# The first three query and key norms of a windowed attention kernel: their roots as a power on GpSimd

## The chip, the cores and the metric

The kernel runs on one core of a Trainium2 chip. The metric is the device time of one execution in microseconds (us). The core has five instruction streams that run side by side: TensorE (PE, with its weight loads PEld), VectorE (DVE), ScalarE (ACT), GpSimd (POOL) and SyncE (SP), which here issues the DMAs.

## The reference

One sequence of 4096 tokens of width 256 goes through windowed attention with 16 heads of 16 columns, then a layer norm, a feed-forward layer with binarized weights, and a second layer norm. What matters here is that each head's query and key are divided by their length:

```python
def _l2norm(t):
    n = jnp.sqrt(jnp.sum(t * t, axis=-1, keepdims=True))
    return t / jnp.maximum(n, EPS)

q = _l2norm(proj(Wq))
k = _l2norm(proj(Wk))
v = proj(Wv)
attn = jnp.einsum('bhqd,bhkd->bhqk', q, k)
...                                   # window of 128 keys, a fading bias, softmax
x = _layernorm(x + attention(x))
x = _layernorm(x + ffn(x))
```

## The kernel before

The tokens are cut into 32 blocks of 128. Block n goes through these stages, each written out by hand in the program of its engine; semaphores join them.

- PE projects queries and keys into one PSUM bank (`project_qk`), 512 columns.
- ACT squares them (`squares`, tile `sq`, L649); DVE sums each head's 16 squares (`sums_of`, tile `ss`, L948) and writes `half`, the sum bounded from below times -0.5 (L875). There are 32 sums in a row: 16 heads of queries and 16 of keys.
- The root: ACT takes the logarithm (L654) and the exponential (L656), which gives a first `rnorm`; DVE improves it by one Newton round of three instructions (`round_of`, L880, L882, L884).
- DVE multiplies the projections by `rnorm` (`normalise_rows`, tile `qkn`, L964).
- ACT writes the rounded 16-bit upper part of `qkn` into `parts` (`high_halves`, L665 queries, L668 keys). What the rounding lost goes beside it: in blocks 0 and 1 POOL subtracts for the queries (L1441) and DVE for the keys (`split_keys`, L927); in later blocks POOL does both (`low_halves`, L1425, L1427). DVE copies the queries' pair (`double`, L921).
- SP issues a transposing DMA from `parts` to `qkT` (`turn_parts`, L274), and PE multiplies queries and keys (`scores`, L391). ACT takes the exponential of the scores (L701), and POOL cuts the window out of them (L1407).

Before the regular steps there is an opening for blocks 0, 1 and 2: the program of each engine writes their stages out one behind the other. On DVE, the sum and `half` of block n+1 stand behind the normalisation of block n, then comes the key split of block n, then the round and the normalisation of block n+1. POOL is given nothing in the opening but two constant matrices and the two subtractions. In the opening one semaphore, `newton`, is raised six times for a root: by `half`, by the logarithm, by the exponential and by the three instructions of the round.

The rows of the page name lines of the kernel before.

Of the kernel before, what the change touches and what calls it, by code (L numbers as in the profile page):

```python
# [11 lines left out]
ALU = mybir.AluOpType  # L12
# [3 lines left out]
P = 128  # L16
# [4 lines left out]
H = 16  # L21
# [11 lines left out]
NORM_EPS = 1e-6  # L33
LN_EPS = 1e-5
QK_SCALE = 2.0 ** 10
# [7 lines left out]
NORM_OPS = 6  # L43
# [56 lines left out]
def count(sem_engine, sem, value):  # L100

    if isinstance(value, int) and value <= 0:
        return
    sem_engine.wait_ge(sem, value)


def norm_base(i, next3):

    return (i + 3) * NORM_OPS if next3 else NB * NORM_OPS + (i - NB + 3) * (NORM_OPS - 1) - 1


def norm_columns(next3, ln):

    return slice(0 if next3 else 2 * H, 2 * H + 1 if ln else 2 * H)


def build(nc, x, xT, wqkvT, woT, w1, w1T, b1c, w2T, b2, out):
    with ExitStack() as ctx:
        def sb(name, shape, dt=F32):
            return ctx.enter_context(nc.sbuf_tensor(name, shape, dt))  # L120

        def sem(name):
            return ctx.enter_context(nc.semaphore(name))
# [28 lines left out]
        ss = sb("ss", [P, 2 * H])  # L152
        half = sb("half", [P, 2 * H + 1])
# [3 lines left out]
        rnorm = sb("rnorm", [P, 2 * H + 1])  # L157
# [14 lines left out]
        yparts = sb("yparts", [P, 2, 2, DC, GB, P], F16)  # L172
        yT = sb("yT", [P, 2, 2, DC, GB, P], F16)
        mv_late = sb("mv_late", [P, LATE, 2])
        late_rstd = sb("late_rstd", [P, LATE])
        resid4 = resid[:].rearrange("p n (k t) -> p n k t", k=DC)

# [41 lines left out]
        qkproj_done, sq_done, ss_done, newton, qkn_done = (  # L219
            sem(n) for n in ("qkproj_done", "sq_done", "ss_done", "newton", "qkn_done"))  # L220
# [26 lines left out]
        znewton, z_ready = sem("znewton"), sem("z_ready")  # L247
        end_seed, end_log, end_guess, end_round, end_root = (
            sem(n) for n in ("end_seed", "end_log", "end_guess", "end_round", "end_root"))
        zlast_sum, rows_by_act, last_row = sem("zlast_sum"), sem("rows_by_act"), sem("last_row")  # L250
        stored = [sem("stored_even"), sem("stored_odd")]

# [391 lines left out]
        def _(act):  # L644
            def squares(n, par):

                act.wait_ge(qkproj_done, n + 1)
                count(act, ss_done, n)
                nc.scalar.activation(sq[:], ps[:, QK[par], :], ACT.Square, scale=1.0 / QK_SCALE).then_inc(sq_done, 1)  # L649

            def root(half_, ln_, y, done, base, seeded):

                act.wait_ge(done, base + seeded)
                nc.scalar.activation(ln_, half_, ACT.Ln, scale=-2.0).then_inc(done, 1)  # L654
                act.wait_ge(done, base + seeded + 1)
                nc.scalar.activation(y, ln_, ACT.Exp, scale=-0.5).then_inc(done, 1)  # L656

            def high_halves(n, par, first=False, again=False):

                act.wait_ge(qkn_done, n + 1)  # L660
                count(act, qk_in[par], 8 * (n - 2 - par) + 16 if not isinstance(n, int) or n >= 2 else 0)
                if again:
                    count(act, again_in, (n - 2) * (16 // XS))
                src = qkn[:, par, :].rearrange("p (h d) -> p h d", d=HD)
                made = nc.scalar.activation(parts[:, par, 0:H, 0, :], src[:, 0:H, :], ACT.Copy)  # L665
                if first:
                    made.then_inc(first_high, 1)
                nc.scalar.activation(parts[:, par, H:2 * H, 0:2, :],  # L668
                                     src[:, H:2 * H, :].unsqueeze(2).to_broadcast([P, H, 2, HD]),
                                     ACT.Copy).then_inc(hi_done, 1)  # L670
# [57 lines left out]
            def norm_of(i, next3, ln):  # L728
                base, cols = norm_base(i, next3), norm_columns(next3, ln)
                if not next3:  # L730
                    act.wait_ge(ln_seed, i - 3)
                root(half[:, cols], lnx[:, cols], rnorm[:, cols], newton, base, 1)
# [12 lines left out]
            act.wait_ge(layout, 4)  # L745
            nc.scalar.activation(fade_parts[:], fade_parts[:], ACT.Exp, scale=-1.0).then_inc(fade_made, 1)
            squares(0, 0)
            norm_of(-3, True, False)
            squares(1, 1)
            high_halves(0, 0, first=True)  # L750
            norm_of(-2, True, False)
            squares(2, 0)
            high_halves(1, 1, first=True)
            norm_of(-1, True, False)
            step(0, 0, strips=False, ln=False, both=False, high_first=True)
            step(1, 1, strips=False, ln=False, squares_first=True)
            step(2, 2, strips=False, ln=False, squares_first=True)
# [114 lines left out]
        def _(dve):  # L872
            def rsqrt_seed(s, half_, eps, op, done, scale=1.0):

                nc.vector.tensor_scalar(half_, s, eps, -0.5 / scale ** 2, op, ALU.mult).then_inc(done, 1)  # L875

            def rsqrt_round(half_, a, b, y, done, base):

                dve.wait_ge(done, base + 3)
                nc.vector.tensor_tensor(a, half_, y, ALU.mult).then_inc(done, 1)  # L880
                dve.wait_ge(done, base + 4)
                nc.vector.tensor_tensor(b, a, y, ALU.mult).then_inc(done, 1)  # L882
                dve.wait_ge(done, base + 5)
                nc.vector.scalar_tensor_tensor(out=y, in0=b, scalar=1.5, in1=y, op0=ALU.add,  # L884
                                               op1=ALU.mult).then_inc(done, 1)
# [54 lines left out]
                                                   fade[:, at, :].unsqueeze(2).to_broadcast([P, H, HD]), ALU.mult)  # L940
                made.then_inc(v_ready, 1)

            def sums_of(n, ln):

                base = norm_base(n - 3, True)
                dve.wait_ge(sq_done, n + 1)
                count(dve, newton, base - NORM_OPS + 1)
                nc.vector.tensor_reduce(ss[:], sq[:].rearrange("p (h d) -> p h d", d=HD), AX.X, ALU.add).then_inc(ss_done, 1)  # L948
                dve.wait_ge(ss_done, n + 1)
                count(dve, qkn_done, n)  # L950
                if ln:
                    dve.wait_ge(ln_seed, n - 6)
                rsqrt_seed(ss[:], half[:, 0:2 * H], (NORM_EPS / QK_SCALE) ** 2, ALU.max, newton)

            def round_of(i, next3, ln):

                cols = norm_columns(next3, ln)
                rsqrt_round(half[:, cols], nt_a[:, cols], nt_b[:, cols], rnorm[:, cols], newton, norm_base(i, next3))

            def normalise_rows(n, par):  # L960

                dve.wait_ge(newton, norm_base(n - 3, True) + NORM_OPS)
                count(dve, lo_done, n - 1)
                nc.vector.tensor_tensor(qkn[:, par, :].rearrange("p (h d) -> p h d", d=HD),  # L964
                                        ps[:, QK[par], :].rearrange("p (h d) -> p h d", d=HD),
                                        rnorm[:, 0:2 * H].unsqueeze(2).to_broadcast([P, 2 * H, HD]),
                                        ALU.mult).then_inc(qkn_done, 1)
# [91 lines left out]
                dve.wait_ge(bound_turned, 1)  # L1059
                nc.vector.tensor_reduce(bound_max[:], turned_at, AX.X, ALU.max).then_inc(bound_max_done, 1)  # L1060

            sums_of(0, False)
            round_of(-3, True, False)
            normalise_rows(0, 0)
            sums_of(1, False)
            split_keys(0)
            round_of(-2, True, False)
            normalise_rows(1, 1)
            dve.wait_ge(first_low, 1)
            sums_of(2, False)  # L1070
            split_keys(1)
            round_of(-1, True, False)
            normalise_rows(2, 0)
            dve.wait_ge(first_low, 2)
            fade_values(0, 0)
# [315 lines left out]
        def _(pool):  # L1391

            nc.gpsimd.iota(idx_i[:], pattern=[[0, 1]], base=0, channel_multiplier=1).then_inc(idx_made, 1)
            nc.gpsimd.memset(id16[:], 0.0).then_inc(id_zero, 1)
            nc.gpsimd.memset(id32[:], 0.0).then_inc(id_zero, 1)
            pool.wait_ge(id_zero, 2)
# [14 lines left out]
            def cut_chunk(i, c, slot, both=True):  # L1411

                own = cut_tile(i, c, slot, 0)
                if both:
                    cut_tile(i, c, slot, 1).then_inc(cut_ready, 1)
                else:
                    own.then_inc(cut_ready, 1)
# [13 lines left out]
            def step(i, slot, next2=True, both=True, low_at=2, behind=None):  # L1431
                for c in range(NC):
                    if next2 and c == low_at:
                        low_halves(i + 2, slot % 2)
                    cut_chunk(i, c, slot, both)
                if behind:
                    behind()

            for n in range(2):
                pool.wait_ge(first_high, n + 1)  # L1440
                nc.gpsimd.tensor_tensor(parts[:, n, 0:H, 1, :], qkn[:, n, 0:D].rearrange("p (h d) -> p h d", d=HD),  # L1441
                                        parts[:, n, 0:H, 0, :], ALU.subtract).then_inc(lo_done, 1)
            step(0, 0, both=False, low_at=0)
            step(1, 1, low_at=1)
            for n in range(2, 5):
# [97 lines left out]
```

## Time and profile before

| what | value |
|---|---|
| time, median of 3 runs | 371.64 us (370.44 to 371.90) |
| the profiled execution's own time | 370.31 us |
| its span in the trace | 368.5 us |
| PE busy | 354.4 us, 96% of the span |
| DVE, ACT, POOL busy | 324.7, 309.8, 273.2 us |
| part of the span that the change touches | about 8.5 to 16.4 us |

The profiled execution is one of its own, with its own time; the span is what lies between its first and last recorded instruction. A row of the timeline gives the start, the duration, the engine, the line, the operation, the tiles written and read with their shapes, and in brackets how long the engine had been idle and what ended that.

### The profile page before, as it was taken

To read this page: it belongs to the slowest core of one execution; us is meant where nothing else is said; L and a number is where in the kernel's file an instruction comes from. 1 tells how busy PE (TensorE), PEld (TensorE's weight loads), DVE (VectorE), ACT (ScalarE), POOL (GpSimd) and SP (SyncE) were. 2 spreads that over 40 slices of the span, in tenths; PEclk is the share of its full clock that TensorE was granted. 3 is DMA by queue.
4 is the path that set the end of the run, shared out by engine and by line. 5 is a ranking of instruction groups with operands and counts; after the bars stand their busy time and mean duration, and the time that the engine had idled before them with its cause. 6 is when DMAs were issued, how large, how long until landed. Compare 5 with 4: busy or idle time off the path is not lost. (4 is left out here: it accounts for less than half of the span.)

```text
span 368.5 us, 13159 instructions
## 1 busy us (share of the span) xinstructions
PE 354.4 (96%) x4461; PEld 244.6 (66%) x4461; DVE 324.7 (88%) x860; ACT 309.8 (84%) x539; POOL 273.2 (74%) x418
## 2 busy tenths in 40 slices
PE   8899999999999999999999999999999999999991
PEld 5555676667767766776776667765666666666780
DVE  5978899898898898898889998869889999999995
ACT  2598898888898898998899999988888898897773
POOL 1189999889989999999999999757474663764330
PEclk9999999999999999999999999999999999999997
DMA  7668854835654655767767863303303413413113
GB/s 221 152 139 183 167 117 89 171 85 115 137 119 89 139 118 110 158 148 164 146 166 137 170 130 62 58 4 59 59 0 60 114 58 58 115 48 68 57 60 114
DMA packets 106885, 40.20 MB, mean 109 GB/s; under 512 B 92128, under 2 KB 105824, under 8 KB 106720
## 3 DMA queue, kind: packets, MB, share of 16 engines
q1 hardware_dynamic: 106848, 39.73, 48.7%
q8 instruction: 20, 0.33, 0.4%
q14 instruction: 17, 0.14, 0.1%
HBM read 12.72 MB, written 4.19 MB: 46 GB/s over the span
## 5 line engine op out<-in xcount | busy, mean ns | idle before, releaser
L1407 POOL TENSOR_SCALAR_AFFINE_SELECT prob<-prob 128x512 f32<-128x512 f32 x252 | 153.0, 642 | 11.3 <-ACT prob L701 11.2
L701 ACT ACTIVATE prob<-ps 128x1024 f32<-128x1024 f32 (+1 forms) x128 | 122.1, 1008 | 12.9 <-PE ps L391 12.9
L552 PE MATMUL ps<-yT,sgn 128*128 128x512 f16 x256 | 61.1, 379 | 0.0
L773 ACT ACTIVATE ps<-ps,bias,alpha 128x512 f32<-128x512 f32 x64 | 47.8, 749 | 15.7 <-PE ps L552 12.5
L422 PE MATMUL ps<-wqkv,xt 128*128 128x512 f32 x124 | 58.7, 596 | 0.1
L1475 POOL TENSOR_TENSOR resid<-z,resid 128x256 f32 (+1 forms) x31 | 22.6, 729 | 46.0 <-DVE z L1191 46.0
L412 PE MATMUL ps<-prob,vdiag 128*17 128x128 f32 x1024 | 51.3, 274 | 0.2
L412 PE MATMUL ps<-prob,vnext 128*17 128x128 f32 x992 | 49.9, 273 | 0.0
L552 PEld LDWEIGHTS ps<-yT,sgn 128*128 128x128 f16 x256 | 25.0, 98 | 22.6
L455 PE MATMUL ps<-wo,oT 128*128 128x256 f32 x128 | 36.2, 405 | 0.1
L391 PE MATMUL ps<-qkT 64*64 64x192 f16 (+2 forms) x1024 | 34.0, 248 | 1.9 <-DMA qkT<-parts 1.4
L431 PE MATMUL ps<-wqkv,xt 128*128 128x256 f32 x128 | 34.4, 391 | 1.3 <-DMA wqkv<-in_wqkvT 0.8
L1427 POOL TENSOR_TENSOR parts<-qkn,parts 128x512 f16<-128x512 f32 x30 | 35.0, 1166 | 0.0
L391 PEld LDWEIGHTS ps<-qkT 64*64 64x64 f16 x1024 | 20.0, 105 | 20.1 <-issue 20.0
L422 PEld LDWEIGHTS ps<-wqkv,xt 128*128 128x128 f32 x124 | 21.2, 190 | 16.2 <-issue 15.4
L586 PE MATMUL ps<-sgn,w 128*128 128x256 f16 x256 | 30.6, 273 | 0.0
L412 PEld LDWEIGHTS ps<-prob,vdiag 128*17 128x17 f32 x1024 | 26.2, 97 | 5.9 <-issue 2.3
L586 PEld LDWEIGHTS ps<-sgn,w 128*128 128x128 f16 x256 | 25.1, 98 | 6.3
L586 PE MATMUL ps<-sgn,prob 128*128 128x256 f16 x240 | 28.5, 273 | 0.1
L412 PEld LDWEIGHTS ps<-prob,vnext 128*17 128x17 f32 x992 | 28.2, 98 | 0.0
L1457 POOL TENSOR_TENSOR yparts<-resid,yparts 128x256 f16<-128x256 f32 (+1 forms) x32 | 21.2, 682 | 8.8 <-ACT yparts L767 8.8
L586 PEld LDWEIGHTS ps<-sgn,prob 128*128 128x128 f16 x240 | 23.4, 98 | 5.6 <-DVE prob L1181 0.3
(119 smaller groups left out, 689.0 us busy)
## 6 DMA issues: line engine op xcount, KB each, us to landing
xt<-in_xT SPq DMA_DIRECT2D x32, 128.0 KB, 2.2
resid<-in_x SPq DMA_DIRECT2D x32, 128.0 KB, 2.2
out_dram<-resid SPq DMA_DIRECT2D x7, 512.0 KB, 2.9
w<-in_w2T SPq DMA_DIRECT2D x1, 1024.0 KB, 8.3
w<-in_w1T SPq DMA_DIRECT2D x4, 256.0 KB, 3.3
w_nat<-in_w SPq DMA_DIRECT2D x4, 256.0 KB, 3.3
wqkv<-in_wqkvT SPq DMA_DIRECT2D x3, 256.0 KB, 4.0
qkT<-parts SPq DMA_TRANSPOSE x39, 4.3
```

The lines of the kernel that those rows point to most:

```text
L391: mm = nc.tensor.matmul(ps[keys, SC + 2 * (c % 2) + hp, 2 * P * t + first:2 * P * t + last], qkT[row, H // 2 + 2 * c + t, slot, keys], row ...
L412: mm = nc.tensor.matmul(ps[32 * m:32 * m + HD + 1, OT, P * c:P * c + P], v, p, start=(n == 0), stop=(n == 1 or not near))
L422: mm = nc.tensor.matmul(ps[:, QK[slot % 2], :], xt[:, slot, k, :], wqkv[:, k, 0:2 * D], start=(k == 0), stop=(k == DC - 1))
L431: mm = nc.tensor.matmul(ps[:, VO, 0:D], xt[:, slot, k, :], wqkv[:, k, 2 * D:3 * D], start=(k == 0), stop=(k == DC - 1))
L455: mm = nc.tensor.matmul(ps[:, VO, D:2 * D], oT[:, k, :], wo[:, k, :], start=(k == 0), stop=(k == DC - 1))
L552: mm = nc.tensor.matmul(ps[:, bank, :], sgn1[:, c, P * k:P * k + P], yT[:, par, a, c, :, :], start=(m == 0), stop=(m == 2 * DC - 1))
L586: mm = nc.tensor.matmul(ps[:, banks[b], 0:D], hid[par][:, a, k, P * b:P * b + P], sgn2[:, k, :], start=(m == 0), stop=(m == 2 * HC - 1))
L701: nc.scalar.activation(to, scored, ACT.Exp, scale=QK_SCALE ** -2).then_inc(exp_done, 1)
L773: nc.scalar.activation(bank, bank, ACT.Gelu, bias=bias1[:, k:k + 1], scale=alpha1[:, k:k + 1]).then_inc(gelu_done, 1)
L1407: return nc.gpsimd.affine_select(out=at, in_=at, compare_op=ALU.is_ge, fill=0.0, base=-near, pattern=[[0, CH], [1 if near else -1, P]], ch ...
L1427: nc.gpsimd.tensor_tensor(parts[:, par, H:2 * H, 2:4, :], src[:, H:2 * H, :].unsqueeze(2).to_broadcast([P, H, 2, HD]), parts[:, par, H:2 * ...
L1475: nc.gpsimd.tensor_tensor(resid[:, m, :], z[:, b, :], resid[:, m, :], ALU.add).then_inc(zsum, 1)
```

## The change

For blocks 0, 1 and 2 the six instructions of the root behind `half` become one on POOL: `rnorm` is the bounded sum to the power -0.5, taken elementwise over 128 x 32 numbers. `half` then holds the bounded sum without the factor -0.5. ACT's logarithms and exponentials and DVE's rounds of these blocks are gone (6 instructions and 9). POOL fills a tile with -0.5 once, and raises `newton` by five with its power, so that everything counts on as before. Block 3 and later keep the old root.

```diff
@@ scalar: the opening
             squares(0, 0)
-            norm_of(-3, True, False)
             squares(1, 1)
             high_halves(0, 0, first=True)
-            norm_of(-2, True, False)
             squares(2, 0)
             high_halves(1, 1, first=True)
-            norm_of(-1, True, False)
@@ vector: sums_of
-                rsqrt_seed(ss[:], half[:, 0:2 * H], (NORM_EPS / QK_SCALE) ** 2, ALU.max, newton)
+                if powered:
+                    nc.vector.tensor_scalar(half[:, 0:2 * H], ss[:], (NORM_EPS / QK_SCALE) ** 2, None,
+                                            ALU.max).then_inc(newton, 1)
+                else:
+                    rsqrt_seed(ss[:], half[:, 0:2 * H], (NORM_EPS / QK_SCALE) ** 2, ALU.max, newton)
@@ vector: the opening
-            sums_of(0, False)
-            round_of(-3, True, False)
+            sums_of(0, False, powered=True)
             normalise_rows(0, 0)
-            sums_of(1, False)
+            sums_of(1, False, powered=True)
             split_keys(0)
-            round_of(-2, True, False)
             normalise_rows(1, 1)
             dve.wait_ge(first_low, 1)
-            sums_of(2, False)
+            sums_of(2, False, powered=True)
             split_keys(1)
-            round_of(-1, True, False)
             normalise_rows(2, 0)
@@ gpsimd
+            nc.gpsimd.memset(minus_half[:], -0.5).then_inc(halves_set, 1)
...
+            def first_root(n):
+
+                pool.wait_ge(newton, norm_base(n - 3, True) + 1)
+                count(pool, qkn_done, n)
+                nc.gpsimd.tensor_tensor(rnorm[:, 0:2 * H], half[:, 0:2 * H], minus_half[:],
+                                        ALU.pow).then_inc(newton, NORM_OPS - 1)
+
+            pool.wait_ge(halves_set, 1)
+            first_root(0)
             for n in range(2):
                 pool.wait_ge(first_high, n + 1)
                 nc.gpsimd.tensor_tensor(parts[:, n, 0:H, 1, :], qkn[:, n, 0:D].rearrange("p (h d) -> p h d", d=HD),
                                         parts[:, n, 0:H, 0, :], ALU.subtract).then_inc(lo_done, 1)
+                first_root(n + 1)
```

On POOL, at the opening of its program, the instructions before are these (the identity matrices `id`, the two subtractions for the queries of blocks 0 and 1, then those of block 2 and the window cuts):

```order
L1394 MEMSET id 128x128
L1395 MEMSET id 128x128
L1398 AFFINE_SELECT id<-id 128x128 x2
L1441 TENSOR_TENSOR parts<-qkn,parts 128x16x16 x2
L1425 TENSOR_TENSOR parts<-qkn,parts 128x16x16
L1427 TENSOR_TENSOR parts<-qkn,parts 128x16x32
```

and now:

```order
L1394 MEMSET minus_half 128x32
L1395 MEMSET id 128x128
L1396 MEMSET id 128x128
L1399 AFFINE_SELECT id<-id 128x128 x2
L1444 TENSOR_TENSOR rnorm<-half,minus_half 128x32
L1451 TENSOR_TENSOR parts<-qkn,parts 128x16x16
L1444 TENSOR_TENSOR rnorm<-half,minus_half 128x32
L1451 TENSOR_TENSOR parts<-qkn,parts 128x16x16
L1444 TENSOR_TENSOR rnorm<-half,minus_half 128x32
L1426 TENSOR_TENSOR parts<-qkn,parts 128x16x16
L1428 TENSOR_TENSOR parts<-qkn,parts 128x16x32
```

A power stands ahead of each of the two subtractions and one behind them, ahead of block 2's.

On DVE, the stretch from the sums of block 1 to the normalisation of block 1 reads before:

```order
L948 TENSOR_REDUCE ss<-sq 128x32
L875 TENSOR_SCALAR half<-ss 128x32
L927 TENSOR_TENSOR parts<-qkn,parts 128x16x32
L921 COPY parts<-parts 128x16x32
L880 TENSOR_TENSOR nt_a<-half,rnorm 128x32
L882 TENSOR_TENSOR nt_b<-nt_a,rnorm 128x32
L884 SCALAR_TENSOR_TENSOR rnorm<-nt_b,rnorm 128x32
L964 TENSOR_TENSOR qkn<-ps,rnorm 128x512
```

and now:

```order
L947 TENSOR_REDUCE ss<-sq 128x32
L953 TENSOR_SCALAR half<-ss 128x32
L926 TENSOR_TENSOR parts<-qkn,parts 128x16x32
L920 COPY parts<-parts 128x16x32
L967 TENSOR_TENSOR qkn<-ps,rnorm 128x512
```

The three instructions of the round are gone, and the key split of block 0 with its copy is all that still stands between `half` and the normalisation.

## Rows read from the trace of the kernel before

**Rows 1.** The page: span, busy time by engine, granted clock in 40 slices

```profile
span 368.5 us, 13159 instructions
...
PE 354.4 (96%) x4461; PEld 244.6 (66%) x4461; DVE 324.7 (88%) x860; ACT 309.8 (84%) x539; POOL 273.2 (74%) x418
...
PEclk9999999999999999999999999999999999999997
```

**Rows 2.** Windows: stretch, length, busy time of each engine, clock, DMA

```profile
17.00:60.00 43.00, 41.38 (x568) 26.44 (x568) 37.43 (x79) 38.05 (x67) 39.12 (x60) 1.00 0.71 149
60.00:200.00 140.00, 139.64 (x2264) 98.22 (x2263) 125.63 (x312) 124.60 (x218) 129.84 (x197) 1.00 0.61 131
```

**Rows 3.** Timeline of DVE and ACT, block 0, from half to the normalisation

```profile
8.35 0.18 DVE L875 TENSOR_SCALAR half<-ss 128x32 f32<-128x32 f32 x1
8.56 0.23 ACT L654 ACTIVATE lnx<-half 128x32 f32<-128x32 f32 x1 [0.97 <-DVE half L875]
9.53 0.19 DVE L884 SCALAR_TENSOR_TENSOR rnorm<-nt_b,rnorm 128x32 f32<-128x32 f32 x1
9.76 0.69 DVE L964 TENSOR_TENSOR qkn<-ps,rnorm 128x512 f32<-128x512 f32 x1
```

**Rows 4.** Timeline of DVE, block 1, from half to the normalisation

```profile
11.08 0.61 DVE L875 TENSOR_SCALAR half<-ss 128x32 f32<-128x32 f32 x1
11.61 0.68 DVE L927 TENSOR_TENSOR parts<-qkn,parts 128x512 f16<-128x512 f32 x1
12.21 0.28 DVE L921 COPY parts<-parts 128x512 f16<-128x512 f16 x1
...
13.07 0.69 DVE L964 TENSOR_TENSOR qkn<-ps,rnorm 128x512 f32<-128x512 f32 x1
```

**Rows 5.** Timeline of DVE, block 2, from half to the normalisation

```profile
14.39 0.61 DVE L875 TENSOR_SCALAR half<-ss 128x32 f32<-128x32 f32 x1
...
15.52 0.28 DVE L921 COPY parts<-parts 128x512 f16<-128x512 f16 x1
...
16.39 0.69 DVE L964 TENSOR_TENSOR qkn<-ps,rnorm 128x512 f32<-128x512 f32 x1
```

**Rows 6.** PE's waits up to 45 us, SP's timeline, and landing of the first two transposes

```profile
PE ps L391 <- DMA qkT<-parts: 1.4, 1, 1.4
...
12.58 5.16 SPq L274 DMA_TRANSPOSE qkT<-parts  x2
...
DMA to landing us min/median/max: 4.3/4.3/4.4
```

**Rows 7.** Timeline of ACT, from the first transpose's landing to block 3's squares

```profile
17.11 0.42 ACT L665 ACTIVATE parts<-qkn 128x256 f16<-128x256 f32 x1 [1.59 <-DVE qkn L964]
...
17.95 1.06 ACT L701 ACTIVATE prob<-ps 128x512 f32<-128x512 f32 x2
19.46 0.60 ACT L649 ACTIVATE sq<-ps 128x512 f32<-128x512 f32 x1 [0.44 <-PE ps L422]
```

**Rows 8.** Timeline of POOL up to 19 us

```profile
10.98 0.67 POOL L1441 TENSOR_TENSOR parts<-qkn,parts 128x256 f16<-128x256 f32 x1 [8.95 <-ACT parts L665]
14.29 0.67 POOL L1441 TENSOR_TENSOR parts<-qkn,parts 128x256 f16<-128x256 f32 x1 [2.64 <-ACT parts L665]
18.20 0.67 POOL L1425 TENSOR_TENSOR parts<-qkn,parts 128x256 f16<-128x256 f32 x1 [3.23 <-ACT parts L668]
```

**Rows 9.** POOL's groups by form: busy us, mean ns, idle before

```profile
L1407 POOL TENSOR_SCALAR_AFFINE_SELECT prob<-prob 128x512 f32<-128x512 f32 x252 | 153.0, 642 | 11.3 <-ACT prob L701 11.2
L1427 POOL TENSOR_TENSOR parts<-qkn,parts 128x512 f16<-128x512 f32 x30 | 35.0, 1166 | 0.0
L1425 POOL TENSOR_TENSOR parts<-qkn,parts 128x256 f16<-128x256 f32 x30 | 20.3, 678 | 8.5 <-ACT parts L668 8.4
...
L1398 POOL TENSOR_SCALAR_AFFINE_SELECT id<-id 128x128 f32<-128x128 f32 x1 | 0.3, 292 | 0.0
```

**Rows 10.** Timeline of DVE, a round's first instruction beside POOL's window cuts

```profile
27.73 0.61 DVE L880 TENSOR_TENSOR nt_a<-half,rnorm 128x32 f32<-128x32 f32 x1
```

More of the change, by code:

```diff
@@ L174, in build @@
         mv_late = sb("mv_late", [P, LATE, 2])
+        minus_half = sb("minus_half", [P, 2 * H])
         late_rstd = sb("late_rstd", [P, LATE])
@@ L249, in build @@
             sem(n) for n in ("end_seed", "end_log", "end_guess", "end_round", "end_root"))
+        halves_set = sem("halves_set")
         zlast_sum, rows_by_act, last_row = sem("zlast_sum"), sem("rows_by_act"), sem("last_row")
@@ L941, in fade_values, with sums_of @@
                 made.then_inc(v_ready, 1)
-            def sums_of(n, ln):
+            def sums_of(n, ln, powered=False):
                 base = norm_base(n - 3, True)
```

## The prediction

> **What bounds the kernel now.** I read the page first: of a span of 368.5 us PE is busy for 354.4, at a granted clock in the top tenth in every slice but the last [rows 1]. The windows say where the rest is: from 60 to 200 us PE is busy for 139.64 of 140 us, from 17 to 60 us for 41.38 of 43 [rows 2]. So behind the opening there is next to no idle time of PE into which a late start could vanish, and none from which an early start could be robbed: what the opening gains or loses at about 17 us, the end gains or loses, nearly one for one. The chain of waits on the page ends before it gets back to the opening, so this is an inference from busy time, not a reading of the chain.
>
> Then the opening. PE stands still for 1.4 us until the first transpose has landed; SP issued it at 12.58, as soon as the copy of block 0 was done, and it took about 4.3 us [rows 4, 6]. ACT stood still for 1.59 us before 17.11 and then rounds block 2 up to the exponentials of 17.95 [rows 7]. So two paths arrive at 17.1 us together: root 0, normalisation 0, key split 0, copy, transpose; and roots 0, 1 and 2 one behind the other on DVE, normalisation 2, rounding of block 2. The first has no slack. The second has 0.44 us, which is ACT's wait for PE's projection of block 3 before the squares at 19.46 [rows 7].
>
> **The change part by part.** I call P the duration of one power on POOL and work out each block in P.
>
> Block 0. Before, `half` ends at 8.53 and the normalisation starts at 9.76, 1.23 us later [rows 3]. Now there are a handover to POOL, the power, and a handover back. For the two handovers I take 0.07 and 0.04 us, from `half`'s end to the logarithm (0.03) and from the round's end to the normalisation (0.04) with some more for POOL [rows 3]. The shift is P + 0.11 - 1.23 = P - 1.12. DVE has nothing else to do meanwhile: the sums of block 1 stand behind the normalisation.
>
> Block 1. `half` ends at 11.69, and DVE goes straight to the key split of block 0 (L927) and the copy, which ends at 12.49 [rows 4]. Here the port matters. `half` took 0.18 us in block 0 and 0.61 in blocks 1 and 2, where it ran against a subtraction on POOL (10.98 to 11.65, 14.29 to 14.96) [rows 3, 4, 5, 8]; and a round's instruction takes 0.61 against the window cuts [rows 10]. So DVE's instructions and POOL's keep each other out. The key split is on DVE as soon as `half` ends, 0.07 us before POOL has its signal, so I take it that the split and the copy go first and the power behind them: 12.49 + P + 0.04 against 13.07 before, a shift of P - 0.54. If POOL gets in ahead of the copy instead, the normalisation comes out much the same, but the copy, and so the first transpose, is late by P as well; for that to decide it must exceed the second path's shift, which it doesn't.
>
> Block 2 is block 1 again: copy end 15.80, normalisation 16.39 [rows 5], P - 0.55.
>
> So the first path shifts by P - 1.12 and the second by 3P - 2.21; less its slack of 0.44 that is 3P - 2.65. The end shifts by the larger. They cross at P = 0.77.
>
> What else is removed or added costs nothing here. ACT loses six lookups of 0.23 us [rows 3], while it idles anyway: the squares of block 1, which stood behind a logarithm, come earlier, but the DVE sum that reads them stays behind normalisation 0. POOL's fill of 32 columns falls into its idle 8.95 us [rows 8]. Behind the last power POOL has the subtractions of block 2, which started at 18.20 after 3.23 us idle [rows 8]; the power ends before the normalisation whose result they need, so they are never held by it.
>
> **The price of P.** No row shows a power. The floor: subtractions of 256 and 512 columns take 678 and 1166 ns [rows 9], so 1.91 ns a column and 0.19 us fixed, and 32 columns come to 0.25 us. A power can't be cheaper than one subtraction. The ceiling: it has to be worked out on POOL as a series of arithmetic steps (take the exponent apart, a polynomial for the logarithm, a product, a polynomial for the exponential, put together), my estimate being 20 to 60 steps. A step costs at least what one more column of a one-input instruction costs, (642 - 292) / 384 = 0.91 ns, at most a subtraction's 1.91 [rows 9]. So 20 steps at 0.91 are 0.77 us and 60 at 1.91 are 3.86 us. I take 35 steps at the cheap rate, since intermediate results need no reading from memory: 0.19 + 32 x 35 x 0.00091 = 1.2 us. The range runs from 0.25 to 3.86.
>
> The Trainium skill speaks against this choice. GPSIMD Engine Reference, section Performance pitfalls for Q7 kernels, says that an fp32 chain in which each step needs the one before pays 4 cycles an element, at a 1.2 GHz clock (section Specifications). No row here shows such a chain. By it my 35 steps would be an estimated 0.19 + 32 x 35 x 0.00333 = 3.9 us, and the sum would be about +9 us instead of +1; rival 2 is that case by rows.
>
> **The sum.** At P = 1.2 the blocks shift by +0.08, +0.66 and +0.65, together +1.39, less 0.44 is +0.95 us. The profiled execution would go from 370.31 to 371.26; it stands 1.33 below the median of the runs, so the median goes from 371.64 to 372.6.
>
> **The rivals.** A measurement of this kernel can tell about 0.5%, 1.86 us, from no change. By 3P - 2.65 that is P = 1.50.
> 1. P from 0.8 to 1.5 (forecast): -0.25 to +1.85, so 371.4 to 373.5. Chance 0.30.
> 2. The power becomes the bound of the opening: P from 1.5 to 3.86, +1.9 to +8.9 us; at P = 2.5 it is +4.85, 376.5. For it: three powers stand one behind the other on the second path, each with DVE waiting. Against it: nothing but my count of steps. Chance 0.28.
> 3. The power is far dearer, worked lane by lane or with its code fetched at first use: at P = 6 it is +15, 387. Nothing in the trace speaks for or against; POOL's first subtraction took 0.67 us like its second [rows 8], so the known code needed no such thing. Chance 0.13.
> 4. The power is cheap, P from 0.25 to 0.8: the first path decides, -0.87 to -0.3, so 370.8 to 371.3. More can't come, because the second path arrives no earlier than the transpose that ACT and PE both need. Chance 0.22, of which 0.04 for something behind the opening falling into place so that it passes 1.86.
> 5. The power shuts DVE out only while it reads, so that it runs beside the key split: blocks 1 and 2 shift by P - 1.27 and P - 1.28, never below -0.54 and -0.55. At P = 1.2 the first path's +0.08 decides, 371.7. For it: arithmetic needs no port. Against it: `half` waited until the subtraction's very end [rows 4, 8]. Chance 0.07. On this the Trainium skill (SBUF — State Buffer, section SBUF: two separate sides) says that the shared port pair is held for the full instruction, so this rival would fall; by that rule the sum stays +0.95.
>
> **The numbers.** Faster by over 0.5%: 0.04. Within 0.5%: 0.30 + 0.18 + 0.07 = 0.55. Slower: 0.28 + 0.13 = 0.41. The range runs from the cheapest price with a little scatter, 370.6, to the dearest bounded one, 371.64 + 8.9 = 380.5; outside stand most of rival 3 and a few hundredths below. The likeliest case alone would have 371.4 to 373.5.
>
> **What would show it.** In the changed kernel: the L1444 rows on POOL give P at once. DVE's normalisations should start at 8.53 + 0.11 + P, then later by 3.31 - 0.54 + P, then by 3.32 - 0.55 + P. In block 1 the power's row should start when the copy's ends, about 12.5 plus block 0's shift; starting at 11.76 plus that shift would be rival 5 or POOL winning the port, told apart by the length of the key split (0.68 us or longer). PE's wait for the first transpose should change by P - 1.12, and ACT's 0.44 us before the squares of block 3 should be gone. The prediction is wrong if P is above 1.5, or if PE's later idle time absorbs a shift that the opening shows.

## The result and the profile after

The changed kernel takes 384.67 us (median of 4 runs, 384.46 to 387.32); the kernel before, on the same chip, 371.26. The ratio on record is 1.039, 95% interval 1.036 to 1.042, which is 14.5 us; the two medians lie 13.4 us apart. Either way it is slower and outside the forecast range of 370.6 to 380.5. The profiled execution's span grew from 368.5 to 383.0 us, by 14.5, and the parts below are parts of that.

The page of the changed kernel: span, busy time by engine, granted clock in 40 slices.

```profile
span 383.0 us, 13151 instructions
...
PE 357.6 (93%) x4461; PEld 246.5 (64%) x4461; DVE 320.7 (84%) x851; ACT 308.0 (80%) x533; POOL 290.0 (76%) x422
...
PEclk9696999999999999999999999999999999999997
```

POOL is busy 16.8 us longer [rows 1]. The timeline of POOL in the opening shows with what:

```profile
8.82 5.44 POOL L1444 TENSOR_TENSOR rnorm<-half,minus_half 128x32 f32<-128x32 f32 x1 [6.73 <-DVE half L953]
15.52 0.67 POOL L1451 TENSOR_TENSOR parts<-qkn,parts 128x256 f16<-128x256 f32 x1 [1.25 <-ACT parts L667]
16.36 5.75 POOL L1444 TENSOR_TENSOR rnorm<-half,minus_half 128x32 f32<-128x32 f32 x1 [0.17 <-issue]
23.36 0.67 POOL L1451 TENSOR_TENSOR parts<-qkn,parts 128x256 f16<-128x256 f32 x1 [1.25 <-ACT parts L667]
24.21 5.75 POOL L1444 TENSOR_TENSOR rnorm<-half,minus_half 128x32 f32<-128x32 f32 x1 [0.17 <-issue]
```

A power over 128 x 32 numbers takes 5.44 to 5.75 us, where the forecast took 1.2 and bounded it at 3.86. The subtractions between them are unchanged at 0.67 [rows 8]. The timeline of DVE in the same stretch answers to [rows 3, 4, 5]:

```profile
14.30 0.69 DVE L967 TENSOR_TENSOR qkn<-ps,rnorm 128x512 f32<-128x512 f32 x1 [5.66 <-POOL rnorm L1444]
14.91 0.68 DVE L947 TENSOR_REDUCE ss<-sq 128x32 f32<-128x512 f32 x1
15.62 0.60 DVE L953 TENSOR_SCALAR half<-ss 128x32 f32<-128x32 f32 x1
16.14 0.68 DVE L926 TENSOR_TENSOR parts<-qkn,parts 128x512 f16<-128x512 f32 x1
16.75 0.34 DVE L920 COPY parts<-parts 128x512 f16<-128x512 f16 x1
22.15 0.69 DVE L967 TENSOR_TENSOR qkn<-ps,rnorm 128x512 f32<-128x512 f32 x1 [5.06 <-POOL rnorm L1444]
...
29.99 0.69 DVE L967 TENSOR_TENSOR qkn<-ps,rnorm 128x512 f32<-128x512 f32 x1 [5.06 <-POOL rnorm L1444]
```

Two things are to be seen. The normalisations stand at 14.30, 22.15 and 29.99, which is 4.54, 9.08 and 13.60 us later than before: 4.5 us a root. And the copy runs from 16.75 to 17.09, in 0.34 us, while the power of 16.36 is under way. The key split ahead of it starts at 16.14, 0.22 us before the power's row, and takes its usual 0.68.

Lining up the 32 normalisations of the two traces in order shows how the loss goes on. The shifts are 4.54, 9.08, 13.60, 13.09, 14.43 us for blocks 0 to 4, then 14.2 to 14.5 for nearly every block up to the last, and 14.47 for the last full scaling of the feed-forward layer at 359 us. So 13.60 us arise at the three roots, 0.51 are given back in block 3, 1.34 are lost anew in block 4, and what stands then stands at the end. The windows of the changed kernel (stretch, length, PE's busy time and records, clock, DMA) show what lies at the fourth step:

```profile
25.00:27.00 2.00, 0.00 (x0) 1.00 0.43 82
27.00:29.00 2.00, 0.00 (x0) 1.00 0.98 181
29.00:31.00 2.00, 0.00 (x0) 0.64 0.00 0
31.00:33.00 2.00, 0.67 (x16) 0.50 0.00 0
33.00:35.00 2.00, 2.00 (x11) 0.50 0.03 8
35.00:37.00 2.00, 2.00 (x19) 0.65 0.45 85
37.00:39.00 2.00, 2.00 (x11) 1.00 1.13 208
```

PE has nothing to do from 24.9 to 32.28 us, since the second half of block 0's scores waits for the exponential, and that for block 2's rounding. At 29.6 us its granted clock falls from 2.4 to 1.2 GHz, and it gets the full clock back only at about 36 us.

### The profile page after: what moved, and what is told of

The parts are those of the page before. It is cut to its first block and busy times, and to the rows that moved or that the text cites. A ratio compares the mean times of both kernels' runs of the same rounds, so it can differ in the third digit from the quotient of the medians.

```text
span 383.0 us, 13151 instructions
## 1 busy us (share of the span) xinstructions
PE 357.6 (93%) x4461; PEld 246.5 (64%) x4461; DVE 320.7 (84%) x851; ACT 308.0 (80%) x533; POOL 290.0 (76%) x422
## 5 line engine op out<-in xcount | busy, mean ns | idle before, releaser
L424 PE MATMUL ps<-wqkv,xt 128*128 128x512 f32 x124 | 60.7, 613 | 5.8 <-DVE qkn L967 5.8
L967 DVE TENSOR_TENSOR qkn<-ps,rnorm 128x512 f32<-128x512 f32 x32 | 22.1, 691 | 17.2 <-POOL rnorm L1444 15.8
L433 PE MATMUL ps<-wqkv,xt 128*128 128x256 f32 x128 | 35.2, 398 | 0.8 <-DVE resid L903 0.4
L667 ACT ACTIVATE parts<-qkn 128x256 f16<-128x256 f32 x32 | 13.5, 420 | 18.6 <-DVE qkn L967 18.6
```

What stands on the lines that cost most here:

```text
L424: mm = nc.tensor.matmul(ps[:, QK[slot % 2], :], xt[:, slot, k, :], wqkv[:, k, 0:2 * D], start=(k == 0), stop=(k == DC - 1))
L433: mm = nc.tensor.matmul(ps[:, VO, 0:D], xt[:, slot, k, :], wqkv[:, k, 2 * D:3 * D], start=(k == 0), stop=(k == DC - 1))
```

## The experiments

**Block 0 alone, block 2 alone.** The first keeps `first_root(0)` and gives blocks 1 and 2 their old root; the second keeps only `first_root(2)`.

```diff
 # block 0 alone
-            sums_of(1, False, powered=True)
+            sums_of(1, False)
             split_keys(0)
+            round_of(-2, True, False)
...                                       # and the same for block 2
-                first_root(n + 1)
 # block 2 alone
-            sums_of(0, False, powered=True)
+            sums_of(0, False)
+            round_of(-3, True, False)
...                                       # and the same for block 1
-            first_root(0)
...
-                first_root(n + 1)
+                if n == 1:
+                    first_root(n + 1)
```

> Block 0 alone takes its root as a power on GpSimd; blocks 1 and 2 keep logarithm, exponential and round. Theory (each power of 5.4 to 5.8 us stands whole on the path to its normalisation, and what the opening loses the end loses): the three normalisations of the opening start 4.5 us late, all three alike; the first transpose is as late and has no slack, so block 3's normalisation is 4.5 late too; the end +4.5 us, and up to 1.3 more if TensorE's clock falls in the longer wait. Rival (the loss comes from powers running beside the key split and fighting for the port, which happens in blocks 1 and 2 alone): block 0's power is harmless beyond its own wait, and the end is clearly less than a third of the whole 14.5 us, under +3.

Measured: 376.32 us, ratio 1.014 (1.011 to 1.016); shifts of the normalisations 4.46, 4.46, 5.53, 6.11 and then 6.1 up to the end. The first two are as expected. The third wasn't: PE's projection of block 2 waits for normalisation 0, and by then PE had the half clock (0.50 in the window of 15 to 19 us), so that it took 3.75 us instead of 1.96 before and held block 2's squares and sums. In the profile of this run:

```profile
9.86 1.13 PE L433 MATMUL ps<-wqkv,xt 128*128 128x256 f32 x4 [1.15 <-DMA wqkv<-in_wqkvT]
...
15.06 3.75 PE L424 MATMUL ps<-wqkv,xt 128*128 128x512 f32 x4 [4.06 <-DVE qkn L969]
...
18.85 0.60 ACT L651 ACTIVATE sq<-ps 128x512 f32<-128x512 f32 x1 [2.18 <-PE ps L424]
19.53 0.69 DVE L949 TENSOR_REDUCE ss<-sq 128x32 f32<-128x512 f32 x1 [1.31 <-ACT sq L651]
```

The rival of the fight for the port falls: one power with no split beside it costs 4.5 us for its wait. The other 1.6 in this profile I put down to the clock; no run of this kernel with the waits filled tests that.

> Block 2 alone takes its root as a power; blocks 0 and 1 as before. Theory: block 2's normalisation starts 4.5 us late, the first transpose is on time, and ScalarE's 0.44 us of slack before the squares of block 3 are eaten: block 3's normalisation and the end +4.0 us, plus up to 1.3 if the clock falls. Rival (a third of the whole for each power, no slack anywhere): +4.8. A second rival, that the step from sums to transposes of block 2 can hide behind the scores of blocks 0 and 1: under +2.

Measured: 376.21 us, ratio 1.013 (1.011 to 1.016); shifts 0.21, 0.29, 4.83, 4.32, 6.43, then 6.4 to 6.5. The first 0.2 to 0.3 is a later start of that execution. So block 2's power costs 4.54, block 3 gives 0.51 back, and block 4 adds 2.1, more than the 1.3 I had allowed; the clock was at half from 22 to 29 us. By their ratios the two single powers cost 5.1 and 4.9 us, and the three together 14.5. The 4.9 is also what the first rival here said (+4.8, no slack); its reason falls, since the 0.51 us of slack is there in the trace. The rivals by which a single power is harmless or can hide fall in both runs.

**The clock.** Matmuls that nothing reads fill PE's two long waits in the changed kernel.

```diff
             project_v(0, 0)
+            pe.wait_ge(consts, 2)
+            keep_warm(22, SC)
             project_qk(2, 2)
...
+                if isinstance(i, int) and i == 0:
+                    keep_warm(30, OT)
                 scores(i, 2, par, slot, both)
```

> The changed kernel with 22 more idle-time matmuls (5.2 us) while TensorE waits for block 0's normalisation and 30 more (7.1 us) while it waits for block 2's; nothing reads them. Theory (1.3 of the 14.5 us are the half clock that TensorE was granted from 30 to 36 us): the granted clock is full from 30 to 36 us, the normalisations of blocks 0 to 3 stand where the changed kernel has them (+4.5, +9.1, +13.6, +13.1), that of block 4 is +13.1 and not +14.4, and the end is 1.3 us earlier than the changed kernel's, about +13.1 against before. Rival (the step from +13.1 to +14.4 is GpSimd's backlog of window cuts or the transposes' landing): it stays, +14.4.

Measured: 383.33 us, ratio 1.033 (1.031 to 1.036), with a span of 381.6 against 383.0. Its windows from 30 us:

```profile
30.00:36.00 6.00, 5.18 (x53) 3.45 (x53) 5.93 (x11) 5.29 (x11) 4.41 (x7) 1.00 0.01 3
```

The clock is full, and the end is earlier than in the changed kernel by 1.4 us in the spans and 1.3 in the medians, as expected. Block 3's normalisation stands at +13.56 instead of the +13.09 that I expected: DVE's round of that block now runs beside POOL's window cuts, and its first instruction takes 0.54 us and not 0.18. Block 4 then adds nothing more (+13.55, against +14.43 in the changed kernel), so the rival by which its step comes from the window cuts or the landing falls. But +13.1 was expected there: up to block 27 the kernel is 0.9 us ahead of the changed one, of which 0.2 is an earlier start, and only in the last scaling of the feed-forward layer are the full 1.4 reached. So by the end the clock accounts for 1.3 to 1.4 of the 14.5 us, and the three powers for the rest; how the last 0.5 of it comes about was not traced.

**The price by size and value.** Extra instructions stand behind POOL's last one; the fragment shows the loop. The rows 0 to 4 of `trial` hold 0.37, 1.0, 0.000015, -0.5 and 2.0, so (0, 3, 32) is 0.37 to the power -0.5 over 32 columns.

```diff
+            for base, power, cols, op in ((0, 3, 32, ALU.subtract), (0, 3, 4, ALU.pow), (0, 3, 8, ALU.pow),
+                                          (0, 3, 16, ALU.pow), (0, 3, 32, ALU.pow), (0, 3, 64, ALU.pow),
+                                          (1, 3, 32, ALU.pow), (2, 3, 32, ALU.pow), (0, 4, 32, ALU.pow)):
+                pool.wait_ge(tested, done)
+                nc.gpsimd.tensor_tensor(trial[:, 5, 0:cols], trial[:, base, 0:cols],
+                                        trial[:, power, 0:cols], op).then_inc(tested, 1)
```

> The kernel before with nine extra GpSimd instructions behind its last one, one after the other, on a tile that nothing else reads: a subtraction of 32 columns; powers of 0.37 to -0.5 over 4, 8, 16, 32 and 64 columns; powers over 32 columns of 1.0 to -0.5, of 0.000015 to -0.5, and of 0.37 to 2.0. The execution's time is longer by their sum and says nothing. Theory (a power is a long series of dependent steps worked for 16 lanes at once): proportional to the columns, about 0.17 us a column and 0.1 to 0.3 fixed, so 4 columns 0.9, 16 columns 2.8, 32 columns 5.4, 64 columns 10.7; the same for every value; the subtraction 0.25. Rival (a large fixed call, for a routine that has to be entered): 4 columns cost over 3 us and 64 under 8. Second rival (branches on the value): 1.0 or the exponent 2.0 cost under half.

The timeline of POOL at the end of this run, in the order of the list; the last row holds two powers together:

```profile
361.64 0.40 POOL L1519 TENSOR_TENSOR trial<-trial 128x32 f32<-128x32 f32 x1
...
362.12 1.02 POOL L1519 TENSOR_TENSOR trial<-trial 128x4 f32<-128x4 f32 x1
363.23 1.76 POOL L1519 TENSOR_TENSOR trial<-trial 128x8 f32<-128x8 f32 x1
365.06 2.90 POOL L1519 TENSOR_TENSOR trial<-trial 128x16 f32<-128x16 f32 x1
368.04 5.43 POOL L1519 TENSOR_TENSOR trial<-trial 128x32 f32<-128x32 f32 x1
373.55 10.55 POOL L1519 TENSOR_TENSOR trial<-trial 128x64 f32<-128x64 f32 x1
384.17 5.43 POOL L1519 TENSOR_TENSOR trial<-trial 128x32 f32<-128x32 f32 x1
389.68 10.94 POOL L1519 TENSOR_TENSOR trial<-trial 128x32 f32<-128x32 f32 x2
```

From 16 columns up a column costs 0.158 to 0.160 us, with about 0.3 us fixed. Powers of 1.0 and 0.37 to -0.5 take 5.43 each; those of 0.000015 to -0.5 and of 0.37 to 2.0 take 10.94 together. So there is no large fixed call and no short way for easy values. The subtraction of 32 columns took 0.40 us, where my floor for P was 0.25; but DVE's addition with two inputs in SBUF, the on-chip memory, ran beside it (361.64 to 361.93), so it is no clean price.

**The port.** That is the forecast's word for what DVE and POOL share when they keep each other out. In the changed kernel the second and third power took 0.31 us longer than the first. Here DVE holds its key splits back until the power has ended.

```diff
             sums_of(1, False, powered=True)
-            split_keys(0)
+            dve.wait_ge(newton, norm_base(-2, True) + NORM_OPS)
+            split_keys(0)
             normalise_rows(1, 1)
...                                       # and the same ahead of split_keys(1)
```

> The changed kernel, with VectorE's key split of blocks 0 and 1 held back until the power beside it has ended. Theory (VectorE's split kept the power from the port for a while, which is why the second and third took 5.75 us and the first 5.44): all three powers take 5.44; the normalisations behind the splits start 0.3 earlier for that and 0.9 later for the split now ahead of them, so each of blocks 1 and 2 is 0.6 later than in the changed kernel, about +1.2 us in the end. Rival (the second and third are longer for another reason, such as their values): they stay at 5.75.

> The changed kernel with the key splits of blocks 0 and 1 held behind the powers, timed. In its one look it was 1.4 us shorter than the changed kernel although block 2's normalisation came 0.9 later. Theory (the stretch of half clock fell ahead of block 3's projection there, and not behind it, which is worth about 1.3): the median is 0.5 to 1.5 us below the changed kernel's 384.67, so 383.2 to 384.2. Rival (the one look was chance): 384.7 + 0.9, 385.6.

The rows of the power in the first of the two runs:

```profile
8.71 5.45 POOL L1446 TENSOR_TENSOR rnorm<-half,minus_half 128x32 f32<-128x32 f32 x1 [6.62 <-DVE half L953]
16.25 5.43 POOL L1446 TENSOR_TENSOR rnorm<-half,minus_half 128x32 f32<-128x32 f32 x1 [0.17 <-issue]
24.58 5.42 POOL L1446 TENSOR_TENSOR rnorm<-half,minus_half 128x32 f32<-128x32 f32 x1 [0.17 <-issue]
```

All three take 5.4 us. So DVE's split and copy cost the power 0.3 us, and it costs them 0.06 (the copy's 0.34 against 0.28). That alone doesn't say what a power does to an instruction that starts after it, for the split had started first. The trace of the run with the sizes does, since DVE's last instructions run beside its powers there:

```profile
361.01 0.58 DVE L1296 TENSOR_SCALAR half<-zmv 128x2 f32<-128x2 f32 x1
...
364.21 0.17 DVE L1296 TENSOR_SCALAR half<-zmv 128x2 f32<-128x2 f32 x1
364.32 0.16 DVE L882 TENSOR_TENSOR nt_a<-half,rnorm 128x2 f32<-128x2 f32 x1
```

The first of them, beside POOL's additions and fills, took 0.58 us. The other two start 1.0 and 1.1 us into the power of 363.23 to 364.99 and take 0.17 and 0.16, as they do in the kernel before, where POOL has nothing left to do. So a power under way doesn't shut DVE out, though these are instructions of two columns only.

The end was another matter: I had expected +1.2 us against the changed kernel, and the one execution of that run took 383.31, 1.4 less. Timed, the kernel takes 384.21 us (ratio 1.036, 1.031 to 1.041), not to be told from the changed kernel's 384.67. In both profiles block 2's normalisation is later than in the changed kernel (+14.46 and +14.73) and the end earlier (+13.1 and +13.6). There PE projects block 3 only after the half clock has set in, and is back at the full one at 33 us instead of 36; that this is the whole reason was argued from the windows, not tested. Nor is it all that differs: the first transpose, which takes 4.4 us in the changed kernel, takes 5.3 in both runs. In the first of them:

```profile
22.71 2.03 SPq L276 DMA_TRANSPOSE qkT<-parts  x1
...
28.12 0.64 PE L393 MATMUL ps<-qkT 64*64 64x64 f16 x16 [6.00 <-DMA qkT<-parts]
```

**The other direction.** What would a faster root have been worth? Three kernels leave out DVE's Newton round, which makes `rnorm` less exact: in blocks 0 to 2, in block 0 alone, and in blocks 0 to 2 with ten more idle-time matmuls ahead of the first scores.

```diff
-            round_of(-3, True, False)
-            round_of(-2, True, False)     # these two stay where block 0 alone is changed
-            round_of(-1, True, False)
...
-WARM_AGAIN = 14
+WARM_AGAIN = 24                           # the third kernel alone
```

> The kernel before without VectorE's Newton round in blocks 0 to 2; logarithm and exponential stay. Theory (the opening passes to the end, the path with block 0's root and the first transpose decides a gain): normalisations -0.7, -1.25 and -1.8 us, first transpose -0.7, block 3's squares and the end -0.7. Rival (a gain is swallowed: another wait, such as that for the weights' transfer or for the projection of block 3, holds the squares of block 3): 0. Second rival (the path of three roots decides): -1.4 or more.

> The kernel before without VectorE's Newton round in block 0 alone, so that the three roots come earlier by one and the same amount. Theory (in the run without all three rounds the first transpose landed no earlier because the second was issued 0.7 us closer behind it and the two shared the queues; here their distance is again 3.3 us): normalisations of blocks 0, 1 and 2 all 0.5 to 0.7 us earlier, first transpose 4.4 us long and landing 0.5 earlier, the end -0.5 if TensorE's clock holds. Rival (the transfer of the second weights and of block 4 holds the first transpose whatever its issue): it takes 4.9 or more and lands at 17.1, the end 0. Second rival (TensorE's longer idle time brings the half clock again): +1 to +2.

> The kernel before without the Newton round in blocks 0 to 2, as in the earlier run, and with 24 instead of 14 idle-time matmuls ahead of the first scores. Theory (the +1.9 to 2.1 us of that run are the half clock from 17 to 21 us, behind 2.2 us of TensorE idle): the clock stays full, the first transpose lands at about 17.35 again, block 3's normalisation is +0.2 to +0.3 and so is the end. Rival (the loss comes from the order on the other engines): it stays at +1.3 for block 3 and +1.9 for the end.

Measured: 371.82 us, ratio 1.003 (1.001 to 1.005); 371.46 us, ratio 1.000 (0.998 to 1.003); 372.42 us, ratio 1.003 (1.001 to 1.005). The normalisations did come earlier, by 0.51, 1.17 and 1.85 in the first and by 0.45 to 0.46 each in the second; the end did not, it came 0 to 0.3% later. PE and ACT in the second:

```profile
17.52 0.42 PE L391 MATMUL ps<-qkT 64*64 64x64 f16 x16 [2.30 <-DMA qkT<-parts]
17.87 3.52 PE L422 MATMUL ps<-wqkv,xt 128*128 128x512 f32 x4
...
17.47 0.42 ACT L665 ACTIVATE parts<-qkn 128x256 f16<-128x256 f32 x1 [2.40 <-DMA qkT<-parts]
```

The first transpose was issued 0.45 us earlier and landed 0.4 us later, 5.3 us after its issue instead of 4.4 [rows 6]. PE waited 2.3 us for it and not 1.4, its clock then stood at half, and block 3's projection took 3.5 us instead of 2. This profiled execution, at 372.18 us, is the second longest of 12; its mean granted clock was 0.990, while 8 of the 12 had 0.993 or more, as 19 of the 23 of the kernel before. So most executions probably kept the full clock, and still their median is no better. My theory that the second transpose crowds the first fell, since their distance was the old one. In the third kernel the clock was full throughout, the transpose took 5.2 us again, and block 3's normalisation stood at +1.07, of which some 0.8 is a later start of that execution: +0.2, as expected, against the +1.26 of the first kernel. But the end was not +0.3: from block 6 on the shifts of the normalisations grow to between 1.5 and 2.9, and the median is no better than the first kernel's. So the clock explains block 3, and not the end. What took its place begins, in this trace, with another slow transpose: the fourth, issued at 28.97, took 5.9 us instead of 4.3, and PE, which had stood still for 1.0 us, went on just behind its landing at 34.90:

```profile
34.99 0.55 PE L391 MATMUL ps<-qkT 64*64 64x192 f16 x16 [1.03 <-issue]
```

Whether that makes the median too is open; this profiled execution is the longest of the 12.

**The load beside the first transpose.** Was it the 1 MB load of the second weights that stretched the transpose? It is issued behind the second transpose here, and DVE's first sum over it is moved behind block 4's normalisation; the second kernel also leaves out block 0's round.

```diff
-            sp.dma_start(w2_t, w2T).then_inc(w2_in, 16)
             load_block(XS, 0)
             turn_parts(0, 0)
             turn_parts(1, 1)
+            sp.dma_start(w2_t, w2T).then_inc(w2_in, 16)
```

> The kernel before, with the 1 MB load of the second weights issued behind the second transpose instead of ahead of block 4's loads, and with VectorE's first sum over them (1.9 us) moved behind block 4's normalisation. Control for the next run. Theory: the first transpose takes 4.3 to 4.4 us as before, since it started as the load ended; VectorE's sum moved from an idle place to a busy one costs 0 to 1 us; 0 to +1 in the end. Rival (the load stretches the transposes of blocks 2 and 3 now): +1 to +2.

> The kernel of the control, without the Newton round of block 0. Theory (in the run without that round alone the first transpose took 5.3 us instead of 4.4 because it was issued while the load of the second weights was still at its end): here it takes 4.4 and lands 0.5 us earlier than in the control, TensorE is idle for no longer, its clock holds, and the end is 0.5 us below the control. Rival (something else ties the landing to about 17.1 to 17.4, for instance block 4's loads): it takes 5 or more, and the end is 0 to +2 against the control.

Measured: 372.28 us, ratio 1.003 (1.002 to 1.005), transpose 4.4 us; and 373.13 us, ratio 1.005 (1.004 to 1.007), transpose 5.2 us. The control is at +1.2 us by its ratio, above the 0 to +1 of the theory and within the rival's +1 to +2, whose reason, stretched transposes of blocks 2 and 3, accounts for 0.2 at most in the trace (4.5 us for block 2's and 4.3 for block 3's). So the load is not the cause of the 5.2. In the traces all four kernels without block 0's round had a first transpose of 5.2 to 5.3 us, and the kernels with an old root or a power there one of 4.4, except the two runs of the kernel with the split held back: 5.3. In these no other load was under way as the transpose was issued (a DMA share of 0.01 in the microsecond before the packets), which speaks against the loads of block 4 as well. In the windows of the DMA its packets move for about 2.7 us whether it takes 4.4 or 5.3; most of the difference lies between them and the landing. What makes it is open. No kernel tried beats the kernel before.

The trace of the second kernel shows one thing more. PE waited 2.3 us for its first transpose, as in the kernel without block 0's round alone, but here the clock stayed full, and block 3's projection took 2.0 us and not 3.5:

```profile
18.20 0.42 PE L391 MATMUL ps<-qkT 64*64 64x64 f16 x16 [2.30 <-DMA qkT<-parts]
18.54 1.98 PE L422 MATMUL ps<-wqkv,xt 128*128 128x512 f32 x4
```

So the length of that wait alone doesn't decide on the clock. And with the full clock block 3's normalisation still stands at +1.03, of which 0.2 is a later start: 0.8 us come from the late landing.

## Why the prediction was wrong

**The price of the power, the step that failed.** The forecast said "the range runs from 0.25 to 3.86" and took 1.2, from 0.19 us fixed and 35 steps at 0.91 ns a column. Measured are 0.3 us fixed and 0.16 us a column, 5.44 us for 32 columns. The same 35 steps would be 4.6 ns each, or at 0.91 ns there would be some 175 of them. Which of the two factors was wrong no run shows. The count was a guess of 20 to 60 without a row behind it, and the rate came from a window cut, without a row to say that a power's steps would run at it; the ceiling of 60 steps at a subtraction's 1.91 ns a column took both for granted. Rival 3 had the size (P = 6, +15 us, chance 0.13). Of its two reasons a code fetch at first use falls, since the first power, 5.44, is not longer than those after it; working lane by lane was not tested. Rival 2 had the path, three powers one behind the other, and too small a P.

On this the Trainium skill (GPSIMD Engine Reference, section Performance pitfalls for Q7 kernels) was nearer: its 4 cycles for each step of a dependent chain gave, with the same guessed count, an estimate of 3.9 us, still 1.5 short of the measured 5.44, but like it above the 1.5 us at which the change counts as slower. That a power is such a chain no run shows.

**Block by block.** Block 0's P - 1.12 gives 4.32 for 5.44, measured 4.54, of which 0.11 is a later `half` and the rest a longer handover: right but for that. For blocks 1 and 2 the forecast's P - 0.54 and P - 0.55 give 4.90 and 4.89 with the power's own 5.44, and 5.2 each with the 5.75 of their rows; measured 4.54 and 4.52. The step "the split and the copy go first and the power behind them" is half right. The split does go first and costs the power its 0.31 us. The power doesn't wait for the copy's end: 17.09 + 5.44 + 0.04 would put the normalisation at 22.57, and it stands at 22.15. Rival 5's P - 1.27 and P - 1.28 give 4.17 and 4.16 for 5.44, and with the 0.31 that the split costs 4.48 and 4.47. What [rows 4] showed, `half` waiting for a subtraction's end, holds after the change too (15.62, 0.60 us), but doesn't carry over to an instruction behind a power.

The Trainium skill (SBUF — State Buffer, section SBUF: two separate sides) gives the shared ports to one of the two engines for its whole instruction, to the one that starts first. That a split which had started first made the power longer agrees with it. That `nt_a`, with two inputs in SBUF, took 0.16 us beginning 1.1 us into a power of 1.76 doesn't: for this pair the measurement decides against the rule.

**The slack and what passes on.** ACT's 0.44 us before block 3's squares was right: 0.51 was given back, and in the run with block 2's power alone again 0.51. That the opening's shift goes through to the end nearly one for one was right for losses: 14.43 us in block 4, 14.47 at the end.

**The missing term.** The forecast has no clock in its sum, although it saw PE waiting. At block 4 of the changed kernel 1.34 us arise behind the half clock; filling the waits with matmuls took that step away and gave back 1.3 to 1.4 at the end. The 1.6 and 2.1 of the kernels with one power are put down to the clock by their traces alone.

The measured shifts add up to 4.54 + 4.54 + 4.52 - 0.51 + 1.34 = 14.43 us. The forecast's own formula 3P - 2.65 gives 13.7 for P = 5.44. That it comes so near is in part luck: it has 0.7 too much for the port, and 0.2 too little for block 0's handovers and 1.3 too little for the clock.

**Rival 4 would probably have failed too.** It gave a cheap power -0.87 to -0.3 us. No run has a cheap power, but those without the round stand for it, since they bring the roots 0.5 us earlier: nothing reached the end, and in their traces the first transpose landed no earlier. The forecast had taken its 4.4 us as fixed.

## What to carry to other kernels

- Where an operation has no row in the trace, guessed steps times the rate of another instruction are no bound; when the price that decides (here 1.5 us) lies inside such a guess, time the operation alone first, behind the last instruction of the kernel, where nine prices cost one run.
- A latency that is put three times in a row on a path with no slack is paid three times, and then the clock of the engine that waits has to be priced as well.
- A gain ahead of a DMA has to be followed to the landing: here 0.5 us earlier at the issue brought nothing at the landing.
- A profile shows one execution. Where it is among the longest of its kernel, as in all four runs without block 0's round, its time and mean clock have to be held against the others before its waits are taken for the kernel's.

## What the runs showed of the hardware

- A power on GpSimd: 0.3 us and 0.16 us a column (128 rows, fp32), whatever the values tried; 32 columns take 5.4 us, over 23 times one of ACT's lookups of 0.23 us.
- A key split of VectorE, begun 0.22 us before a power on GpSimd, kept its 0.68 us and, with its copy, made the power 0.31 us longer. VectorE's instructions that began inside a power kept their speed or nearly so: a copy 0.34 us against 0.28, one with two inputs in SBUF and two columns 0.16 us. Beside a subtraction of GpSimd `half` took 0.60 against 0.18 us.
- PE's granted clock went from 2.4 to 1.2 GHz in waits of 7.3 us and 5.5 us in the changed kernel, and behind one of 2.3 us in the profiled execution without block 0's round. It stayed full behind 1.4 us in the kernel before, and behind 2.3 us again in the kernel with the load moved as well.
- The same transposing DMA took 4.4 us from issue to landing in the traces of seven kernels and 5.2 to 5.3 in those of five others, and neither the neighbouring transpose nor the 1 MB load was the reason.
